# Moving a 128x1024 multiplication of the weight dequantization from GpSimd to VectorE

## The reference, cut to what matters

```python
GROUP = 16
def _dequant(q, scale):
    w = q.astype(jnp.float32) / 7.5 - 1.0
    return w * jnp.repeat(scale, GROUP, axis=1)

def _qlora_linear(x, q, scale, bias, la, lb):
    w = _dequant(q, scale)
    base = jnp.einsum('btd,od->bto', x, w) + bias
    lora = jnp.einsum('btr,or->bto', jnp.einsum('btd,rd->btr', x, la), lb)
    return base + lora
...
x = _layernorm(x + _L0_attn_ref(x, ...), axis=-1)
x = _layernorm(x + _L0_ffn_ref(x, ...), axis=-1)   # three blocks of two _qlora_linear each
```

## Time and profile before

| | |
|---|---|
| median of 3 runs | 2848.84 us (2847.83 to 2851.02) |
| the profiled execution | 2847.45 us |
| its span on the slowest core (core 2) | 2845.9 us |
| spans of the 8 cores | 2809.7 to 2845.9 us |
| busy: TensorE, VectorE, ScalarE, GpSimd | 58%, 34%, 35%, 6% |
| granted TensorE clock, mean | 0.788 of full speed on core 2 |

### The profile page before, as it was taken

How to read it: one execution, slowest core, us unless ns; L and a number is a source line. 1 busy time by engine, 2 the same in 40 slices (tenths; PEclk the granted TensorE clock), 3 DMA queues, 4 the chain that set the end, 5 groups by cost and what they waited for, 6 DMA issues and landing times.

```text
span 2845.9 us, 21744 instructions; the slowest of 8 cores (2809.7 to 2845.9 us)
## 1 busy us (share of the span) xinstructions
PE 1644.3 (58%) x6750; PEld 689.0 (24%) x6880; DVE 978.8 (34%) x1001; ACT 988.0 (35%) x1472; POOL 169.2 (6%) x148
## 2 busy tenths in 40 slices
PE   0899880199986011111586556665666575566863
PEld 0344330044432000000232222222222232222321
DVE  1113435212343511112235350542615327242362
ACT  0321121041204011111444545445454544455444
POOL 0000000000000133333000000000000000000000
PEclk9999995599998555555798877888878797688985
DMA  5210123520021455556301004100051000501001
GB/s 170 77 59 16 45 74 150 164 85 23 16 81 38 182 172 170 171 172 197 109 30 59 1 27 152 59 30 30 4 174 59 30 30 0 178 30 60 30 1 59
DMA packets 72543, 228.63 MB, mean 80 GB/s; under 512 B 6768, under 2 KB 7024, under 8 KB 66032
## 3 DMA queue, kind: packets, MB, share of 16 engines
q1 hardware_dynamic: 61680, 181.09, 19.8%
q0 software_dynamic: 10752, 46.14, 4.1%
HBM read 181.07 MB, written 46.14 MB: 80 GB/s over the span
## 4 chain that ended last, share of the span: by engine, by line
PE 46%; ACT 15%; DMA 13%; DVE 11%; issue 8%; POOL 2%; PEld 2%; DVEq 1%; SPq 1%; PEldq 1%; ACTq 0%; POOLq 0%
PE ps L755 23%; PE ps L258 8%; DMA PL<-sc_t 5%; PE ps L370 4%; PE ps L313 4%; ACT PL L931 2%; PE ps L735 2%; POOL PL L602 2%; PEld ps L446 2%; DMA PL<-wq_t 2%; DMA PL<-xt 2%; PE ps L983 2%; DMA weffs<-PL 2%; DVE PL L923 2%; DVE PL L921 2%
## 5 line engine op out<-in xcount | busy, mean ns | idle before, releaser
L755 PE MATMUL ps<-PL 128*128 128x512 bf16 x3000 | 732.8, 397 | 272.6 <-ACT PL L931 237.6
L755 PEld LDWEIGHTS ps<-PL 128*128 128x128 bf16 x3072 | 310.4, 102 | 673.7 <-issue 348.0
L258 PE MATMUL ps<-PL 128*128 128x512 bf16 x1004 | 225.1, 384 | 211.0 <-DVE PL L211 206.6
L631 PE MATMUL ps<-PL 32*128 32x512 bf16 x48 | 28.1, 586 | 377.6 <-DVEq L649 239.0
L899 DVE TENSOR_TENSOR e2s<-e2s,m2s 128x512 f32<-128x512 f32 x32 | 22.1, 692 | 552.4 <-ACT e2s L891 552.4
L778 ACT ACTIVATE PL<-ps,fb 128x512 bf16<-128x512 f32 x192 | 131.9, 687 | 165.7 <-PE ps L737 165.4
L258 PEld LDWEIGHTS ps<-PL 128*128 128x128 bf16 x1024 | 100.6, 99 | 335.0 <-issue 218.2
L791 DVE SCALAR_TENSOR_TENSOR PL<-ps,fb,PL 128x512 f32<-128x512 f32 x192 | 144.2, 751 | 91.0 <-PE ps L755 90.5
L983 PE MATMUL ps<-eye,PL 128*128 128x128 f32 x256 | 90.3, 436 | 139.9 <-ACT PL L997 74.5
L446 PE MATMUL ps<-PL 128*128 128x512 bf16 x627 | 141.8, 387 | 21.1 <-ACTq L171 20.2
L735 PE MATMUL ps<-PL,ones_b 128*128 128x512 bf16 x192 | 76.8, 400 | 118.2 <-ACT sqd L781 118.2
(11 more groups left out here) (75 smaller groups left out, 1630.5 us busy)
## 6 DMA issues: line engine op xcount, KB each, us to landing
PL<-weffs SPq DMA_DIRECT2D x24, 2048.0 KB, 8.9
PL<-xt SPq DMA_DIRECT2D x32, 1024.0 KB, 5.9
PL<-qw_t SPq DMA_DIRECT2D x48, 512.0 KB, 5.1
PL<-sc_t SPq DMA_DIRECT2D x48, 512.0 KB, 6.2
x1s<-PL POOLq DMA_DIRECT2D x16, 1024.0 KB, 4.1
PL<-x1s SPq DMA_DIRECT2D x64, 256.0 KB, 8.0
out<-PL POOLq DMA_DIRECT2D x32, 512.0 KB, 4.0
weffs<-PL POOLq DMA_DIRECT2D x48, 256.0 KB, 2.6
```

The lines of the kernel that those rows point to most:

```text
L258: last = e.matmul(ps[bank][:], bfv(area + c * 512, 1024)[:, s * 128:(s + 1) * 128], xtbf[:, c * 2048 + tc * 512:c * 2048 + (tc + 1) * 512] ...
L755: last = e.matmul(ps[bank][:], bfv(WSL[sl], 8192)[:, c * 1024 + s * 128:c * 1024 + (s + 1) * 128], src_mv[:, c * 512:(c + 1) * 512], start ...
```

## The change

The multiplication by the scales moves from GpSimd to VectorE, just ahead of the two additions, with a wait on its own semaphore between them. VectorE takes over the waits for ScalarE and for the loads. It now counts three "ve" steps for each chunk instead of two. GpSimd is left with the stores: each waits for the addition of its own chunk, and no longer stands behind the product of the chunk two later.

```diff
-            gp_bq = cnt["gp"]
-            dq_ve = {c: lac + 2 * (c + 1) for c in range(EC)}
-            dq_gp = {c: gp_bq + c + 1 for c in range(EC)}
+            dq_ve = {c: lac + 3 * (c + 1) for c in range(EC)}
...
             @blk.gpsimd
             def _(e):
                 for c in range(EC):
-                    wt(e, "se", se_bq + c + 1)
-                    wt(e, "gq%d" % (c % 2), qldb[c % 2] + 32 * (c // 2 + 1))
-                    if c >= 2:
-                        wt(e, "ve", dq_ve[c - 2])
-                    inc(e.tensor_mul(fv(O_TMP + (c % 2) * 1024, 1024),
-                                     fv(O_TMP + (c % 2) * 1024, 1024),
-                                     fv(O_SCL + (c % 2) * 1024, 1024)), "gp")
-                    if c >= 2:
-                        inc(e.dma_start(out=weffs.ap()[w, c - 2],
-                                        in_=bfv(34816 + (c % 2) * 512, 1024)),
-                            "sw%d" % (c % 2), 16)
-                for c in range(EC - 2, EC):
                     wt(e, "ve", dq_ve[c])
                     inc(e.dma_start(out=weffs.ap()[w, c],
                                     in_=bfv(34816 + (c % 2) * 512, 1024)),
...
                 for c in range(EC):
                     bank = 4 + 2 * (c % 2)
-                    wt(e, "gp", dq_gp[c])
+                    wt(e, "se", se_bq + c + 1)
+                    wt(e, "gq%d" % (c % 2), qldb[c % 2] + 32 * (c // 2 + 1))
                     wt(e, "pe", pe_bq + c + 1)
                     wt(e, "sw%d" % (c % 2), swb[c % 2] + 16 * (c // 2))
+                    inc(e.tensor_mul(fv(O_TMP + (c % 2) * 1024, 1024),
+                                     fv(O_TMP + (c % 2) * 1024, 1024),
+                                     fv(O_SCL + (c % 2) * 1024, 1024)), "ve")
+                    chain(e, "ve")
                     e.tensor_add(bfv(34816 + (c % 2) * 512, 1024)[:, 0:512],
                                  fv(O_TMP + (c % 2) * 1024, 512), ps[bank][:])
```

More of the change, by code:

```diff
@@ L650, in dequant_w @@
             assert cnt["ve"] == dq_ve[EC - 1]
-            assert cnt["gp"] == dq_gp[EC - 1]
             w_sw_marks.append((cnt["sw0"], cnt["sw1"]))
```

## The result

The changed kernel takes 2769.15 us (median of 8 executions, 2767.2 to 2854.08); the kernel before was at 2848.34 beside it. The ratio is 0.9725, 95% interval 0.9711 to 0.9739: 2.8% faster, 79 us. The forecast was 2780 us with a range of 2760 to 2808.

The account below looks back on a forecast made before the run. The prediction took the dequantization stage as a loop of latencies: 17 x (15.4 - R), with a round R of 11.36 us, saves 68.5 us, 2847.45 to 2779.0; with 1.4 for the median, say 2780 us, range 2760 to 2808.

Parts of the forecast that it names:

- What bounds the stage: Dequantization of the six weights: a loop of latencies with no resource full, 63.2 us a tensor over the first five.
- The product: Scale product on VectorE: 1.23 us instead of 2.34 on GpSimd, with gaps of 0.26 before and 0.10 after.
- The store at nothing: VectorE's wait for the chunk's store, issued beside the slot's next load: costed at nothing, about 2 us of cover.
- The loads at 7.3 us: SyncE's chunk loads, issue to arrival: 6.5 us plus 0.8 for the other slot's store.
- The round and the tensor: Dequantization loop: a slot's round of 11.4 us, first round 12.5, odd slot 2.7 later, a tensor 50.8 against 63.2.
- The stretch before the first product: From the last tensor's last loads to the network's first product: set by bytes, left at 27.5 us.
- The sum: Five tensors plus the last: 17 x (15.4 - R), R being the round, a gain of 68.5 us.
- A sign that did not show: Spans of all cores were to shorten by about as much, since each has the same loop.
- A: Rival, chunk loads: slots drift apart, loads take 5.4 us, round 9.5, gain 101, about 2747 us; chance 0.10.
- B: Rival, chunk loads or stores: denser traffic stretches loads to 9.2 us, round 13.3, gain 36, 2813 us; chance 0.08.
- C: Rival, SBUF interface shared by VectorE and GpSimd: store issue lengthens the product, 9 us less gain, 2789 us; chance 0.04.
- D: Rival, dequantization loop: slower through DMA latency, loads over 11.3 us; with 12 us a loss of 11, 2859; chance 0.03.

Follow-up runs that it names:

- The store's place: Kernel before, product still on GpSimd, with the store of chunk c-2 queued ahead of the product of chunk c: 2799.0 us, ratio 0.983.
- the second product: Changed kernel with one more VectorE product of the same operands per chunk, into an unused area: 2804.3 us.
- the four slots: Four load slots instead of two, on the changed kernel whose next-tensor loads already wait only for their own slot: 2715.7 us.
- the run with two stores: Changed kernel with each bf16 chunk stored a second time, to another DRAM tensor, VectorE waiting for both: 2802.5 us, ratio 0.984.
- the early loads: Changed kernel with the loads of the network's first tile and first weight (4.2 MB) issued before the last tensor's: 2775.3 us.
- the run with the held-back store: Changed kernel, product on VectorE, but each store issued only after the product of the chunk two later: 2862.4 us, ratio 1.006.

## Why the prediction was right, step by step

**What bounds the stage.** Right. The store's place, the second product and the four slots all show a loop of latencies with room in every engine and in DMA.

**The product.** 1.23 forecast, 1225 ns measured, minimum 1224, maximum 1227. The gaps 0.26 and 0.10 were 0.30 and 0.11.

**The store at nothing.** Right, with one wait of 4.0 us in 48. The cover was thinner than the 2 us of the prediction, though. The store goes out 0.47 us after the load and lands 6.3 us later (median), and VectorE asks for it after 6.70 + 1.06 + 0.30 = 8.1 us: about 1.3 us of cover. It was also the larger part: the store's place alone gave 47 of 79 us. My sum did not show that, since it put product and store into one round. By the runs the two edits are not additive at all: -47 for the store, +16 for the product, -79 for both.

**The loads at 7.3 us.** Near. On core 5 the chunks 2 to 7 needed 6.70 on average, from 5.7 to 8.0. But the tensor's end hangs on the odd slot alone, and this one had 7.3, 7.1 and 8.0 in the first tensor and 7.15 over all six, against 6.2 in the even slot. So its rounds of 11.4 us are those of the forecast. The prediction gave one load time to both slots. The 0.8 us for a second store's bytes was measured as 0.85.

**The round and the tensor.** A tensor was 49.3 us, not 50.8. The term that was mis-sized is the first round: 12.5 forecast, 11.15 measured (976.02 to 987.17), since the first loads arrived after 5.8 us and not 7.0. I had taken these from core 2, the slowest, and its first loads were late in every tensor: 7.6 us on average, against 5.5 on core 0. That is 12 of the 32 us between these two cores at the first product. Core 0 of the kernel before had 5.0 in the same place: its timeline, first load and first arrival:

```profile
969.44 0.35 SPq L588 DMA_DIRECT2D PL<-qw_t  x1
...
974.49 1.28 ACT L620 ACT_TABLE_LOAD   x1 [53.88 <-DMA PL<-sc_t]
```

Over five tensors that is 7 us. Two smaller errors nearly cancel: the odd slot followed 3.1 us behind and not 2.7, and the last chunk's loads needed 6.6 us and not 7.3 (mean of five tensors). What made these arrivals late on one core and not on another was not settled; no run varied it alone.

**The stretch before the first product.** 27.5 forecast, 24.5 measured: 3 us. This isn't a gain of the change. Over the 8 cores the stretch was 20.7 to 27.5 us before, 23.4 on average, and 22.3 to 25.1 after, 23.9 on average; the forecast had taken the longest. That it is set by bytes is shown by the run with two stores (29.3) and by that with the early loads (13.8).

**The sum.** From the forecast of the first product, 1358.7 - 68.5 = 1290.2, to the measured 1284.2: +5.2 for a stage that began later on core 5 than on core 2, -7.4 for five tensors, -1.0 for the last, -3.0 for the stretch. The stage alone was 11.4 us shorter than forecast; that the first product came only 6 us early is in part luck, since core 5 happened to start the stage 5 us later. The other 5 of the 11 us lie outside the stage: 1.8 after the first product, and the median that came out 1.9 below the profiled time (2771.08) where I had added 1.4.

**A sign that did not show.** The spans of all cores should have become shorter by about as much. In the two profiled executions they shortened by 45 us (core 0) to 94 (core 2), 71 on average: the change also brought the cores closer together, which the sum, made for the slowest core, had not said.

**The rivals.** A (loads of 5.4 us) did not happen; by its sum the time would have been 2747. The figure of the Trainium skill that stood beside it ("DMA: Bandwidth & Descriptors", section "Anatomy of one DMA", an estimate of 4.4 us) is given there for a DMA issued by GpSimd, and these loads are SyncE's; none of the chunks 2 to 7 on core 5 needed less than 5.7. B (13.3 us a round) did not happen either; the run with two stores, at 2802, shows how near it is. C, the shared interface: the product takes 1224 to 1227 ns in all 48 cases, also in those with a store issue inside it, as at 987.64 above, and that issue took 0.54. No sign of it. D did not happen for the changed kernel, but it happened in the run with the held-back store, by a mechanism that I had seen only in passing ("behind the waiting instruction on VectorE stands the other slot's chunk") and priced at nothing. Had the diff left the store where it was, the forecast by my steps would have been a gain of 23 us, and wrong in sign.

## What to carry to other kernels

An operation's move to a faster engine also moves what stood behind it in the old queue, and puts it ahead of something in the new one. Price these first: here the store behind the product was worth 47 us by itself, and the product without it lost 16. In a double-buffered loop that waits mostly for arrivals, ask how much is in flight before asking which engine is faster: here more slots and buffers gave as much again as the change, 2769 to 2690.

## What the runs showed of the hardware

A GpSimd store issue beside a VectorE product of two SBUF tensors took its usual 0.54 us (six times on core 5); beside VectorE's casts it was held (five times, 1.03 us each). The changed kernel, core 5, at the end of the first and of the last tensor:

```profile
1024.97 0.68 DVE L571 CAST PL<-PL 32x1024 bf16<-32x1024 f32 x1 [0.21 <-issue]
1025.35 1.03 POOL L597 DMA_DIRECT2D weffs<-PL  x1 [5.95 <-DVEq L640]
1025.58 0.68 DVE L572 CAST PL<-PL 32x1024 bf16<-32x1024 f32 x1
...
1272.06 0.54 POOL L597 DMA_DIRECT2D weffs<-PL  x1 [5.69 <-DVEq L640]
```

The store at 1025.35 took 1.03 us, until the casts were over; the last tensor's last store, at 1272.06, had no cast beside it and took 0.54. In the run with the early loads, on core 1, a store issue at 1285.18 took 2.10 us beside a cast of 2.29 (from 1284.87). Of the two cases that the Trainium skill names ("GPSIMD Engine Reference", section "Key points"), contention beside VectorE instructions in a 2-port mode and beside those with two SBUF inputs, the traces bear out the first, if casts run in that mode (one of 128x2048 took 1227 ns, a product of the same size 2292), and not the second. This is seen on store issues only: no arithmetic on GpSimd ran beside such a product here.
